# Cross-attention and spline network on one core: the last four tiles in another order, and the placing of cells split between GpSimd and VectorE

## What is computed

```python
x = x + xattn(layernorm(x), ctx_2048, seg, ...)          # 16 heads, 8 sequences
h = layernorm(x)                                         # input of the network
xn = layernorm(h) * ln_gamma + ln_beta
tile_idx = best tile (of 64) in the best cluster, by signs of xn     # one per token
x_slice = xn[tile's 16 columns]
tile_min, tile_max = minimum and maximum of x_slice over all tokens of a tile
u  = clip((x_slice - mn) / (mx - mn + 1e-8), 0, 1 - 1e-6)
gi = floor(u * 16)                                       # the cell
delta = (bases[tile, j, gi] + slopes[tile, j, gi] * (u * 16 - gi)) * output_scale[tile]
x = x + h + (delta written into the tile's 16 columns)
```

## Time and profile before

| | us |
|---|---|
| median of 3 runs | 3157.5 (3157.19 to 3158.14) |
| the profiled execution, its own time | 3158.58 |
| its span | 3156.8 |
| PE busy | 3049.6 (97%) |
| DVE busy | 2040.1 (65%) |
| ACT busy | 1519.8 (48%) |
| POOL busy | 697.6 (22%) |

### The profile page before, as it was taken

How to read it: one execution, slowest core, us unless ns; L and a number is a source line. 1 busy time by engine, 2 the same in 40 slices (tenths; PEclk the granted TensorE clock), 3 DMA queues, 4 the chain that set the end, 5 groups by cost and what they waited for, 6 DMA issues and landing times.

```text
span 3156.8 us, 40175 instructions
## 1 busy us (share of the span) xinstructions
PE 3049.6 (97%) x13962; PEld 2379.5 (75%) x13962; DVE 2040.1 (65%) x4424; ACT 1519.8 (48%) x2977; POOL 697.6 (22%) x520
## 2 busy tenths in 40 slices
PE   7999999999999999999999999999999999999984
PEld 4788768887688867888678886888768887788861
DVE  2555637776477756777477773777647775577766
ACT  2665525554355434555355552654435554455543
POOL 5222241111310131111411104111141112211126
PEclk9999999999999999999999999999999999999985
DMA  6654445444444445444454444544454444544421
GB/s 208 200 172 166 165 153 191 144 144 155 170 144 144 132 137 200 138 135 135 159 195 132 135 133 157 200 143 132 144 177 150 142 129 150 184 125 142 144 82 4
DMA packets 173191, 472.85 MB, mean 150 GB/s; under 512 B 36401, under 2 KB 64689, under 8 KB 152385
## 3 DMA queue, kind: packets, MB, share of 16 engines
q1 hardware_dynamic: 167920, 469.41, 45.0%
q0 software_dynamic: 5072, 0.88, 0.6%
HBM read 369.33 MB, written 67.31 MB: 138 GB/s over the span
## 4 chain that ended last, share of the span: by engine, by line
PE 85%; DVE 5%; issue 3%; POOL 3%; DMA 2%; ACT 1%; SPq 0%; DVEq 0%; POOLq 0%; ACTq 0%
PE psC L2006 10%; PE psD L1997 10%; PE psE L2006 9%; PE psA L1928 8%; PE psT L1984 6%; PE psB L1937 5%; PE psA L1897 5%; PE psS L1965 4%; PE psD L1948 4%; PE psS L1971 3%; PE psS L1967 3%; PE psS L1966 3%; PE psS L1968 3%; PE psB L1897 3%; PE psA L1919 2%
## 5 line engine op out<-in xcount | busy, mean ns | idle before, releaser
L1069 ACT ACTIVATE exps_ring<-exps_ring,neg_max 128x512 f32<-128x512 f32 x512 | 370.9, 724 | 421.9 <-DVE neg_max L1387 421.2
L1387 DVE CUSTOM_DVE_ANT_0 exps_ring<-psS,mask 128x512 f32<-128x512 f32 x512 | 353.2, 690 | 289.1 <-PE psS L1971 283.7
L1080 ACT ACTIVATE probsT_hi<-psT 128x512 fp32r<-128x512 f32 x472 | 282.4, 598 | 337.5 <-PE psT L1984 335.8
L1075 ACT ACTIVATE exps_ring<-exps_ring,row_sum_inverse 128x512 f32<-128x512 f32 x512 | 369.7, 722 | 60.8 <-DVE row_sum_inverse L1393 60.8
L1399 DVE TENSOR_TENSOR probsT_lo<-psT,probsT_hi 128x512 fp32r<-128x512 f32 x472 | 323.8, 686 | 54.4 <-ACT probsT_hi L1080 52.6
L2006 PE MATMUL psC<-w_o_pair,attn_hi 128*128 128x512 f32 x1024 | 340.0, 413 | 0.7 <-DVE attn_lo L1405 0.7
L2006 PE MATMUL psE<-w_o_pair,attn_hi 128*128 128x512 f32 x896 | 295.2, 410 | 0.0
L1984 PE MATMUL psT<-ident,exps_ring 128*128 128x128 f32 x1888 | 283.2, 272 | 5.7 <-DVE probsT_lo L1399 4.7
L1984 PEld LDWEIGHTS psT<-ident,exps_ring 128*128 128x128 f32 x1888 | 228.3, 140 | 76.7 <-issue 26.1
L1928 PE MATMUL psA<-q_c_hi,w_uq_ring 128*128 128x512 f32 x768 | 258.6, 391 | 0.7 <-DVE rope_term L1329 0.7
L1965 PE MATMUL psS<-k_hi,q_hi 128*128 128x512 f32 x512 | 203.2, 397 | 6.0 <-DVE q_lo L1364 4.5
(11 more groups left out here) (339 smaller groups left out, 6308.2 us busy)
## 6 DMA issues: line engine op xcount, KB each, us to landing
w_o_pair<-w_o_split SPq DMA_DIRECT2D x112, 1024.0 KB, 5.3
w_uq_ring<-w_uq_split SPq DMA_DIRECT2D x114, 384.0 KB, 3.7
w_uv_quad<-w_uv_split SPq DMA_DIRECT2D x29, 1024.0 KB, 4.9
w_uk_ring<-w_uk_split SPq DMA_DIRECT2D x114, 256.0 KB, 2.7
w_qr_sorted<-w_qr_split SPq DMA_DIRECT2D x29, 768.0 KB, 4.3
x_stage<-in_x_dram SPq DMA_DIRECT2D x32, 512.0 KB, 5.9
x_stage<-in_ctx_dram SPq DMA_DIRECT2D x32, 512.0 KB, 4.0
acc<-in_x_dram SPq DMA_DIRECT2D x32, 512.0 KB, 5.4
```

Of the source, the lines that this page charges most:

```text
L1069: act.activation(E[:, qt, :], E[:, qt, :], ACT.Exp, scale=-1.0, bias=mx[:, i % 2, qt:qt + 1], accum_out=rs[:, i % 2, qt:qt + 1]).then_inc( ...
L1075: act.activation(E[:, qt, :], E[:, qt, :], ACT.Copy, scale=ri[:, i % 2, qt:qt + 1]).then_inc(s_prob, 1)
L1387: dve.tensor_tensor_reduce(E[:, qt, :], psS[qt % 2][:, :], mask[:, qt, :], -SCALE, BIG, ALU.add, ALU.min, mx[:, i % 2, qt:qt + 1]).then_in ...
```

## The change

For the last four tiles:

- Tiles 1 and 3 of the last output projection go to psA and psB, tiles 0 and 2 to psC and psD (`last_banks`). `out_last(0)` and `out_last(1)` both stand before the wait for the old one-hots.
- `stages_end` has tile 1 in psC and psD and tile 3 too. The old one-hots (`old_bank`) use psT, psE and, for the last two groups, psS[1]. The four new one-hots have semaphores of their own (`s_thot`, `s_thc`), and gamma and beta take turns in psE and psS[0].
- PE and ACT have another order, shown below.

In the tail:

- The first comparison on DVE covers 3 tiles instead of 4; ACT's groups are 5, 8, 8 and 8 tiles.
- `token_limits(0)` comes before the fourth spline row. The limits of tiles 16 to 31 lie side by side in psT.
- Tiles 8 to 15 are placed by POOL (`place_second`), 13 instructions ahead of the first scatter. As POOL reads no PSUM here, ACT copies their limits to SBUF (`lims`) before its first group of squares.
- Tiles 16 to 31 are placed by DVE in one pass, after the total of tile 11. `place`'s indices are a function of their own; those of tiles 0 to 7 come after the first pick.
- `first_of_deltas`: 0, 1, 2, 3, 4, 6, 8, 12, ... becomes 0, 1, 3, 5, 8, 12, 14, 16, 18, 20, 24, 28.

```diff
+        s_thot, s_thc = sem("end_onehot_turned"), sem("end_onehot_copied")
...
+        s_lcopy, s_pcell, s_pidx = sem("limits_copied"), sem("pool_cells"), sem("pool_indices")
...
-        def limit_bank(g):
-            return (psC, psB, psT, spare)[g]
-
-        stages_end = [(psS[0], psS[1]), (psS[0], psS[1]), (psC, psD), (psS[0], psS[1])]
-        first_of_deltas = [0, 1, 2, 3, 4, 6] + list(range(8, NTOK, 4))
+        def gamma_beta_bank(t):
+            return (spare, psS[0])[t % 2]
+
+        old_bank = [psT, psE, psT, psE, psT, psS[1], psS[1]]
+        c_end = (B - 1) * CN + TT // 2 + 4 * (PAIRS - 1)
+        d_end = (B - 1) * DN + NQ * DQ - 1
+
+        def last_banks(t):
+            if t % 2:
+                return (psA, fullA, freeA, B * AN + t // 2), (psB, fullB, freeB, B * BN + t // 2)
+            return (psC, fullC, freeC, c_end + t // 2), (psD, fullD, freeD, d_end + t // 2)
+
+        def limit_cols(g):
+            return (psC, psB, psT, psT)[g][:, (64 if g == 3 else 0):(128 if g == 3 else 64)]
+
+        stages_end = [(psS[0], psS[1]), (psC, psD), (psS[0], psS[1]), (psC, psD)]
+        first_of_deltas = [0, 1, 3, 5, 8, 12, 14, 16, 18] + list(range(20, NTOK, 4))
+        firsts = 3
+        lims = E[:, 3, 128:192].rearrange("p (k s c) -> p k s c", s=2, c=4)
         prod = [cosT[:, :], sinT[:, :], rt[:, :], ends[1][2][:, 0:HALF]]
-        rows_ring = [psD, psS[0], psS[1], psA]
+        rows_ring = [psD, psS[1], psA, psS[0]]
...
+            def place_second():
+                mid = slice(8, 16)
+                u, cell, part, f = fu[:, mid], fg[:, mid], fl[:, mid], fin[:, mid]
+                pool.wait_ge(s_lcopy, 1)
+                c = Chain(pool, s_pcell, 0)
+                c.do(pool.tensor_tensor(f, lims[:, :, 0, :], lims[:, :, 1, :], ALU.add))
+                low, inverse = [f[:, :, n:n + 1].broadcast_to([P, 8, SLICE]) for n in range(2)]
+                c.do(pool.tensor_tensor(u, xsl[:, mid, :], low, ALU.subtract))
+                c.do(pool.tensor_scalar(u, u, 0.0, None, ALU.max))
+                c.do(pool.tensor_tensor(u, u, inverse, ALU.mult))
+                c.do(pool.tensor_scalar(u, u, 1.0 - 1e-6, float(GRID), ALU.min, ALU.mult))
+                c.do(pool.tensor_scalar(cell, u, ROUND, None, ALU.add))
+                c.do(pool.tensor_scalar(cell, cell, ROUND, None, ALU.subtract))
+                c.do(pool.tensor_tensor(part, cell, u, ALU.subtract))
+                c.do(pool.tensor_scalar(part, part, 0.0, None, ALU.is_gt))
+                c.do(pool.tensor_tensor(cell, cell, part, ALU.subtract))
+                pool.tensor_tensor(part, u, cell, ALU.subtract).then_inc(s_pcell, 1)
+                c = Chain(pool, s_pidx, 0)
+                c.do(pool.tensor_tensor(idxf[:, mid], f[:, :, 3], tokb[:, mid], ALU.add))
+                c.do(pool.tensor_copy(idxi[:, mid], idxf[:, mid]))
+
+            place_second()
...
-            onehot_turned(0, 1, 2)
+            onehot_turned(0, 1)
             end_normed_first()
+            onehot_turned(2, 3)
             end_sign(0)
+            onehot_turned(4)
             end_sign(1)
+            end_onehot_turned(0)
             end_sign(2)
-            onehot_turned(3)
+            end_onehot_turned(1)
             end_sign(3)
-            onehot_turned(4, 5, 6)
-            end_onehot_turned(0)
-            end_onehot_turned(1)
+            onehot_turned(5)
             end_onehot_turned(2)
+            onehot_turned(6)
             end_sum(0)
             end_onehot_turned(3)
             for t in range(1, TT):
                 end_sum(t)
 
-            for n, (lo, hi) in enumerate(((4, 8), (8, 16), (16, 24), (24, 32))):
-                act.wait_ge(s_cell, lo // 8 + 1)
+            act.wait_ge(s_fin, 2)
+            act.activation(lims, limit_cols(1).rearrange("p (k s c) -> p k s c", s=2, c=4), ACT.Copy).then_inc(s_lcopy, 1)
+            for n, (lo, hi) in enumerate(((firsts, 8), (8, 16), (16, 24), (24, 32))):
+                if lo == 8:
+                    act.wait_ge(s_pcell, 11)
+                else:
+                    act.wait_ge(s_cell, 1 if lo < 8 else 2)
...
-                dve.wait_ge(s_fin, g + 1)
-                src = limit_bank(g)[:, 0:64]
+                dve.wait_ge(s_fin, g + n)
+                src = limit_cols(g) if n == 1 else psT[:, 0:64 * n]
...
-                c.do(dve.tensor_tensor(idxf[:, rows], f[:, :, 3], tokb[:, rows], ALU.add))
+
+            def first_cells():
+                dve.wait_ge(s_tz, TT)
+                dve.wait_ge(s_cell, 1)
+                cells = fg[:, 0:firsts].rearrange("p k (j a) -> p (k j) a", a=1)\
+                    .broadcast_to([P, firsts * SLICE, GRID])
+                ramp = gramp.rearrange("p (a g) -> p a g", a=1).broadcast_to([P, firsts * SLICE, GRID])
+                dve.tensor_tensor(eqb[:, 0:firsts * 256].rearrange("p (k g) -> p k g", g=GRID), cells, ramp,
+                                  ALU.is_equal).then_inc(s_eq0, 1)
+
+            def indices(g, n):
+                rows = slice(8 * g, 8 * (g + n))
+                c.do(dve.tensor_tensor(idxf[:, rows], fin[:, rows, 3], tokb[:, rows], ALU.add))
...
+                if k == 8:
+                    dve.wait_ge(s_pcell, 11)
+                elif kk == 0:
+                    dve.wait_ge(s_cell, 1 if g == 0 else 2)
...
-            place(0)
+            place(0, 1)
+            first_cells()
             pick(0)
+            indices(0, 1)
             for k in range(NTOK):
                 if 0 < k < NTOK - 1:
                     pick(k + 1)
@@ -1859,8 +1912,9 @@
                     deltas(first_of_deltas[ends_of_deltas.index(k + 1)], k + 1)
                 if k == 0:
                     pick(1)
-                if k in (3, 9, 15):
-                    place((k + 3) // 6)
+                if k == 11:
+                    place(2, 2)
+                    indices(2, 2)
...
+                elif g == 5:
+                    pe.wait_ge(s_tsign, 24)
+                elif g == 6:
+                    pe.wait_ge(s_ge, 6)
...
-                elif t == 2:
-                    pe.wait_ge(freeC, B * CN)
-                    pe.wait_ge(freeD, B * DN)
+                elif t == 1:
+                    pe.wait_ge(freeC, c_end + 2)
+                    pe.wait_ge(freeD, d_end + 2)
                 else:
-                    pe.wait_ge(s_tsign, 8 if t == 1 else 16)
+                    pe.wait_ge(s_tsign, 8 * (t - 1))
...
+                if t == 0:
+                    pe.wait_ge(s_ge, 5)
+                else:
+                    pe.wait_ge(s_thc, t)
+                pe.transpose(psTb[0:NT, 0:P], oh4[:, t, :], identb[:, :]).then_inc(s_thot, 1)
 
             def end_gamma_beta(t):
-                if t > 0:
-                    pe.wait_ge(s_tile[t - 1], 11)
-                pe.wait_ge(s_ge, NTOK // 4 + t)
-                pe.matmul(spare[:, 0:2 * SLICE],
+                if t == 0:
+                    pe.wait_ge(s_ge, 4)
+                elif t == 1:
+                    pe.wait_ge(s_tsign, 24)
+                else:
+                    pe.wait_ge(s_tile[t - 2], 11)
+                pe.wait_ge(s_thc, t + 1)
...
-                out_end(B - 1, t, 0)
-                out_end(B - 1, t, 1)
+                for half, (ps, full, free, n) in enumerate(last_banks(t)):
+                    if t == 0:
+                        pe.wait_ge(s_wo[half], 16 * PAIRS * B)
+                        pe.wait_ge(freeD, pos_av(B - 1, NQ - 1, HQ - 2) + 1)
+                    pe.wait_ge(free, n)
+                    split = pos_av(B - 1, NQ - 1, HQ - 1) + 1 if t == 0 and half == 0 else None
+                    project(ps, 1, half, t, split).then_inc(full, 1)
...
+            out_last(1)
             pe.wait_ge(s_ohin, 16)
             turn_onehot(0)
             turn_onehot(1)
-            out_last(1)
+            out_last(2)
             turn_onehot(2)
-            out_last(2)
+            turn_onehot(3)
             end_turn(0)
             out_last(3)
+            turn_onehot(4)
             end_turn(1)
             end_keys(0)
             end_turn(2)
-            turn_onehot(3)
             end_keys(1)
+            end_turn_onehot(0)
             end_turn(3)
-            turn_onehot(4)
+            end_gamma_beta(0)
             end_keys(2)
-            turn_onehot(5)
-            turn_onehot(6)
-            end_turn_onehot(0)
-            end_keys(3)
-            end_gamma_beta(0)
             end_turn_onehot(1)
             end_gamma_beta(1)
+            turn_onehot(5)
+            end_keys(3)
             end_turn_onehot(2)
             end_gamma_beta(2)
+            turn_onehot(6)
+            end_turn_onehot(3)
+            end_gamma_beta(3)
             pe.wait_ge(s_spl[1], 1)
             pe.wait_ge(s_tsign, 8 * TT)
-            end_turn_onehot(3)
-            end_gamma_beta(3)
-            for k in range(4):
+            pe.wait_ge(s_ge, 7)
+            for k in range(3):
                 spline_row(k)
```

(4 more changed lines are left out.)

53 lines of the change are left out of this document (21 added, 32 removed).

## The result

| | before | changed |
|---|---|---|
| median, us | 3157.82 (6 runs, 3155.77 to 3159.3) | 3145.34 (6 runs, 3142.19 to 3146.86) |
| ratio | | 0.9962, interval 0.9952 to 0.9972 |
| profiled execution | 3158.58 | 3145.69 |
| its span | 3156.8 | 3143.9 |

The change is faster by 12.5 us by the medians, or 0.38% by the ratio. 3144.9 was forecast, with a range of 3141.5 to 3150.5; the measured 3145.34 lies inside it.

A forecast was written before the change was run, and what follows sets the result against it. GpSimd's run of 32 scatters closes the kernel, bound by its start and by late deltas. Gains of 6.2 us (last four tiles) and 6.4 us (tail) sum to 12.6, from the median 3157.5 to 3144.9 us; range 3141.5 to 3150.5.

The forecast's parts named there:

- What bounds the tail: Tail: the first scatter's start, and whether deltas keep up with GpSimd's scatters at 1.85 us a tile, set the end.
- First term: Last four tiles: tile limits ready 6.2 us earlier, at 3066.2 instead of 3072.43; bounds 4 and 7.7 us.
- the two paths tie within 0.3 us: Last four tiles: VectorE's path ends at 3063.7, that of ScalarE and TensorE at 3064.0, so any slip shows in full.
- Second term: Tile limits to first scatter: 12.6 us, bounds 9.9 and 16.4, with GpSimd's thirteen instructions; 3.4 us more than before.
- Third term: Deltas in the tail: last scatter starts 71.0 us after the tile limits instead of 77.4, 6.4 us gained.
- The one late group: Tail: deltas of four tiles from tile 20 on come at 50.4 against 49.9 us; scatters lose about 0.8 us once.
- the deltas keep up everywhere: Rival, tail: scatters never starve, the last starts 70.2 us after the tile limits, time 3144.1 us; chance 17%.
- The tile stage: Rival, last four tiles: the stage gives half, tile limits only 3 us earlier, time 3147.9 us; chance 17%.
- GpSimd and VectorE held each other up: Rival, before the first scatter: GpSimd's thirteen instructions each cost double, 5 to 6 us more, time 3149.7 us; chance 14%.
- The slower case: Rival, before the scatters: GpSimd's thirteen instructions take 20.7 us, 1.6 us each, costing more than the gains; chance 2%.

The follow-up runs named there:

- e4: Changed kernel with six more chained one-input 128x128 operations on GpSimd ahead of the first scatter; median 3149.59 us, ratio 0.9975.
- e3: Changed kernel with the placing of tiles 8 to 15 back on VectorE, after the total of tile 2; median 3149.67 us, ratio 0.9973.
- e6: Changed kernel with ScalarE's copies of the turned one-hots of tiles 0 and 1 behind the signs of tiles 2 and 3; median 3145.91 us, ratio 0.9961.
- e7: Changed kernel with GpSimd's placing started only after VectorE's first comparison; ran once, 3148.87 us with the profiler.
- e8: Changed kernel with ScalarE's one-hot of tiles 16 to 23 made in two groups of four; median 3145.3 us.

## Why the prediction held, step by step

- **What bounds the tail.** Right: the scatters' 1.85 us each and the start of the first. e4 shows it (3.33 us in front, 2.98 at the end), e3 the other side (3.9 us earlier in front, 3.36 later at the end).
- **First term, 6.2 us.** Measured 5.76. ScalarE's waits were drawn too long (1.2 against 0.90 and 1.00 us), and by e6 they cost 0.2 us. The step that was off is on VectorE's path: GpSimd's product for tile 0 was to end near 3050.7. It ended at 3050.47, which is 3051.24 with the 0.77 us of the earlier attention added, and the reduction was 0.5 us late with it. The front of that path came forward by 0.5 us where I drew 1. Its cause is one that the prediction left out. GpSimd makes this product only behind the layer norm of tile 3, which starts with VectorE's addition of tile 3, and that waits for TensorE's last products (0.67 us). Counted from the attention the addition came from 15.62 to 15.10 us, so 0.52 earlier, and TensorE's wait for the output weights, 0.45 us where it was 0.20, took about 0.25 of what it could have gained. (VectorE's addition of tile 1, forecast 1.3 us earlier, came 0.3 earlier with its first half and 1.1 with its second, as VectorE was at the statistics of tile 0 before.) The rest of the path, 11.54 us by my sum, took 11.57. That the two paths tie within 0.3 us is borne out by e6.
- **Second term.** GpSimd started at T0 + 4.83 (5.3 forecast), took 7.29 us (6.8), and its first scatter began 0.67 us behind that (0.5), at T0 + 12.78 (12.6). Three errors of up to half a microsecond partly cancel, which is luck; the one with a mechanism is the first instruction, 0.95 us where I had 0.2, by the lock of e7. The prices that I took from a slope and from two shapes were right to 0.06 us, but for the operation with two scalars (0.1 more).
- **Third term.** T0 + 70.95 against 71.0; the later first scatter (0.18) and the shorter wait (0.27) cancel here too. The one late group is the forecast one, with 0.53 us for 0.8, and VectorE's wait in front of tile 16 was 2.31 us (2.3 forecast). e8 shows its cause: ScalarE's one-hot of eight tiles.
- **Rivals.** That the deltas keep up everywhere would have needed 0.5 us more: near, and reached by e8. The tile stage gave 93% of its term, not half (the sum of that rival takes off 3.2 us, where half is 3.1). GpSimd and VectorE held each other up once, for 0.70 us, not at every instruction; in the rest of that stretch VectorE's picks read PSUM. The slower case asked 1.6 us an instruction, and they average 0.49 (6.41 us busy in 13).
- **How near the total is.** The mechanism and the terms hold to half a microsecond. That the median lies 0.4 us from the forecast is better than the runs can tell, since six runs of the changed kernel spread over 4.7 us: part of it is luck. Of the 12.9 us between the two profiles, 0.77 come from the attention stage, which nothing touched and no run explains; the section on what was not expected shows how far that wanders.
